# A mixing and decoding kernel: the first weights loaded in row halves, PSUM banks permuted, decode steps moved earlier, and VectorE making twelve casts in the first sweep

## What is computed

```
attn = einsum('ds,td->st', w1, w2) * sparse_mask
y    = gelu(einsum('bds,st->bdt', x, attn) + b2)        # exact gelu
x    = layernorm(x + y)
mask = norm(x) > 64                                     # per token
w_l, w_h = dequant(qweight, lut4, 4 bits), dequant(qweight, lut8, 8 bits)
x    = layernorm(x + where(mask, x @ w_h.T, x @ w_l.T) + bias)
```

## Time and profile before

| what | us |
|---|---|
| median of 3 runs | 336.0 (335.06 to 337.29) |
| the profiled execution | 336.07 |
| its span, first to last instruction | 334.3 |
| TensorE busy | 301.7 (90%) |
| VectorE busy | 194.5 (58%) |
| ScalarE busy | 185.5 (55%) |
| GpSimd busy | 104.3 (31%) |
| mean granted TensorE clock | 0.956 of full |

### The profile page before, as it was taken

One profiled execution on the slowest core, in us unless ns is written; L12 is line 12 of the kernel. 1 busy time (PEld: TensorE's weight loads), 2 busy tenths in 40 slices (PEclk: granted clock), 3 DMA queues, 4 the chain that ended last, 5 costly groups with the idle time before them and its releaser, 6 DMA issues.

```text
span 334.3 us, 5046 instructions
## 1 busy us (share of the span) xinstructions
PE 301.7 (90%) x1907; PEld 263.6 (79%) x1907; DVE 194.5 (58%) x347; ACT 185.5 (55%) x246; POOL 104.3 (31%) x179
## 2 busy tenths in 40 slices
PE   5899478989996779999999999999999999999970
PEld 2788375656664579999999999999999878878870
DVE  0668857436879577889966766640315434534361
ACT  1656653447887967897857887942124545121210
POOL 3000000322323237779888630000013232322220
PEclk9899877999997959999999999999999999999996
DMA  7999616799987592000111111111905877444232
GB/s 246 371 384 361 225 60 220 223 228 296 218 139 128 80 158 56 32 33 31 38 43 33 38 45 35 60 47 36 304 10 190 259 267 237 176 147 159 94 125 73
DMA packets 27183, 49.35 MB, mean 148 GB/s; under 512 B 2320, under 2 KB 11792, under 8 KB 27152
## 3 DMA queue, kind: packets, MB, share of 16 engines
q1 hardware_dynamic: 22800, 40.56, 35.0%
q0 software_dynamic: 4352, 8.39, 14.7%
HBM read 36.36 MB, written 12.58 MB: 146 GB/s over the span
## 4 chain that ended last, share of the span: by engine, by line
PE 64%; issue 12%; SPq 6%; POOL 6%; DMA 4%; DVE 3%; ACT 2%; POOLq 0%; DVEq 0%
PE acc L536 18%; PE acc L538 18%; PE acc L537 18%; POOL z L1329 5%; PE acc L519 4%; DMA q_low<-in_qbits 4%; SPq L250 3%; PE acc L461 2%; PE acc L451 1%; PE acc L415 1%; ACT x_hi L666 1%; SPq L254 1%; PE acc L431 1%; PE acc L433 0%; PE acc L432 0%
## 5 line engine op out<-in xcount | busy, mean ns | idle before, releaser
L536 PE MATMUL acc<-lin,zz 128*128 128x256 f32 (+2 forms) x424 | 130.9, 309 | 0.3 <-POOL lin L1337 0.3
L538 PE MATMUL acc<-lin,zz 128*128 128x256 f32 (+2 forms) x424 | 130.3, 307 | 0.0
L537 PE MATMUL acc<-lin,zz 128*128 128x256 f32 (+2 forms) x424 | 130.1, 307 | 0.0
L536 PEld LDWEIGHTS acc<-lin,zz 128*128 128x128 f32 x424 | 80.7, 190 | 4.7 <-issue 0.6
L537 PEld LDWEIGHTS acc<-lin,zz 128*128 128x128 f32 x424 | 80.8, 191 | 4.0
L538 PEld LDWEIGHTS acc<-lin,zz 128*128 128x128 f32 x424 | 80.7, 190 | 4.1
L692 ACT ACTIVATE leaf<-planes,lut,flip 128x1024 f32<-128x1024 uint8 x56 | 67.6, 1234 | 0.0
L948 DVE COPY_PREDICATED leaf<-planes,leaf 128x1024 f32<-128x1024 uint8 x32 | 43.1, 1346 | 12.5 <-ACT leaf L692 12.0
L1329 POOL DMA_DIRECT2D z<-in_xr x16 | 19.7, 1257 | 97.3 <-ACT z L674 97.3
L785 ACT ACTIVATE junk<-rows,cols 128x1024 bf16<-128x1024 f32 x15 | 17.2, 1149 | 41.3 <-POOL cols L1303 41.3
L415 PE MATMUL acc<-w,w 128*128 128x272 f32 (+1 forms) x128 | 31.5, 412 | 4.1 <-DMA w<-in_w1b 4.1
(11 more groups left out here) (105 smaller groups left out, 429.8 us busy)
## 6 DMA issues: line engine op xcount, KB each, us to landing
z<-in_xt SPq DMA_DIRECT2D x16, 512.0 KB, 8.8
z<-in_xr POOLq DMA_DIRECT2D x16, 512.0 KB, 6.9
out_rows<-rows SPq DMA_DIRECT2D x15, 512.0 KB, 2.9
w<-in_w2b SPq DMA_DIRECT2D x4, 1024.0 KB, 9.9
w<-in_w1b SPq DMA_DIRECT2D x8, 512.0 KB, 9.4
out_rows<-parts SPq DMA_DIRECT2D x32, 128.0 KB, 1.8
rows<-out_rows SPq DMA_DIRECT2D x16, 256.0 KB, 2.8
off_band<-in_mask_rest SPq DMA_DIRECT2D x8, 448.0 KB, 4.2
```

Source lines behind the costliest of these rows:

```text
L536: nc.tensor.matmul(bank, hi, w_hi, start=k == 0, stop=False)
L537: nc.tensor.matmul(bank, hi, w_lo, start=False, stop=False)
L538: last = nc.tensor.matmul(bank, lo, w_hi, start=False, stop=k == KB - 1)
```

## The change

- The first strip's weights (w2's first quarter, w1's block 0) are loaded in two halves of rows, and strip 0 begins with the first half. q_low is loaded as blocks 0 to 3 right behind the first half and blocks 4 to 7 after the second pair of x, instead of blocks 0, 1 and the rest. x of group 1 is loaded without the two waits.
- The mask band, the excess operands and the warm-up tile move to addresses 128 to 140 KiB, where lin's first part comes later; so lin_hi(0), lin_lo(0) and the memsets of ones wait for their last readers.
- The banks are permuted: units 0 to 3 use banks 4 to 7, units 4 to 7 banks 0 to 3, strips 2 and 3. The turned block 0 is in banks 0 and 1.
- The excess strip stands behind the turn of block 0, ahead of strip 7. Group 0 is mixed in the order of the others. Block 1 is turned behind group 3 and not inside it; later turns stand one or two tiles later. The squares run three tiles ahead at first.
- 24 decode steps stand in the strips (22 before), 9 in the mixing (12 before), 33 in the first sweep (32), 30 in the second. In a group they stand behind gelu 0 and gelu 3 on ScalarE, ahead of the x_lo of pair 0 and of pair 2 on VectorE.
- Group 0's z pairs are made in groups 2 and 3. VectorE makes x_hi of group 0's pairs 0 and 2, and z_hi of groups 1 to 3, in the first sweep's tiles 0 to 10, where before ScalarE made z_hi, six pairs of it in the mixing.

```diff
     EARLY_PARTS = 2 * TILES
-    STATS_AHEAD = 1
+    STATS_AHEAD = 3
...
     DECODE = LEAVES + 3
-    EARLY_STEPS = [5, 2, 2, 2, 2, 3, 3, 3]
-    UNIT_STEPS = [n % 2 for n in range(18)] + [1, 1, 1, 0, 0, 0]
-    FIRST_STEPS = [2] * TILES
-    MIX_Z = {(2, 0): (0, 0), (2, 2): (0, 1), (2, 4): (0, 2), (3, 0): (0, 3), (3, 2): (1, 0), (3, 4): (1, 1)}
-    FIRST_Z = [((1 + n // PAIRS, n % PAIRS),) for n in range(2, 3 * PAIRS)] + [()] * 6
-    SECOND_STEPS = [2] * 15 + [1]
+    EARLY_STEPS = [6, 3, 3, 3, 3, 3, 2, 1]
+    MIX_STEPS = [(2, 1), (2, 1), (1, 0), (2, 0)]
+    MIX_Z = {2: ((0, 0), (0, 1)), 3: ((0, 2), (0, 3))}
+    FIRST_Z = [((1, 0), (1, 1)), ((1, 2),), ((1, 3),)] + [((2 + n // PAIRS, n % PAIRS),) for n in range(2 * PAIRS)] + [()] * 5
+    FIRST_STEPS = [1] + [2] * 11 + [3, 2, 3, 2]
+    SECOND_STEPS = [2] * 15 + [0]
...
     TURN_AFTER_STRIP = 6
-    TURN_IN_MIX = {3: 1}
-    TURN_IN_FIRST = {4: 2, 9: 3, 15: 4}
+    TURN_IN_FIRST = {5: 2, 11: 3, 15: 4}
...
         eye = eye2[:, P:2 * P]
-        UNIT_BANKS, GRAM_BANKS, SUM_BANK = (0, 1, 2, 3, 4, 7, 5, 6), (4, 5), 7
-        STRIP_BANKS, EXCESS_BANK = (5, 6), 7
+        UNIT_BANKS, GRAM_BANKS, SUM_BANK = (4, 5, 6, 7, 0, 1, 2, 3), (4, 5), 7
+        STRIP_BANKS, EXCESS_BANK = (2, 3), 7
...
+            def load_first(rows, signal):
+                sp.dma_start(w2[:, rows, 0:D // W2_PARTS], w2b[0][:, rows, :]).then_inc(signal, 16)
+                sp.dma_start(w1[:, 0, rows, :], w1b[0][:, rows, :]).then_inc(signal, 16)
...
-            for n in range(W2_PARTS):
+            load_first(slice(0, KB // 2), w_first)
+            load_q(0, slice(0, HALF_BLOCKS))
+            sp.dma_start(lut[:, :, :], lut4).then_inc(tables_loaded, 16)
+            sp.dma_start(b2[:, :], b2c).then_inc(tables_loaded, 16)
+            load_first(slice(KB // 2, KB), w_loaded[0])
+            load_w2(1)
+            load_w1(1)
+            load_band(0)
+            load_w1(2)
+            for n in range(2, W2_PARTS):
...
                     load_w1(b)
-                    if b == 0:
-                        load_q(0, slice(0, 2))
-                        sp.dma_start(lut[:, :, :], lut4).then_inc(tables_loaded, 16)
-                        sp.dma_start(b2[:, :], b2c).then_inc(tables_loaded, 16)
-                        load_band(0)
             load_band(1)
-            load_x(0, 0)
...
             sp.dma_start(band_e[0:EXCESS, :, :, :], mask_e).then_inc(e_loaded, 16)
+            load_x(0, 0)
             load_xe(0)
-            load_q(1, slice(2, KB))
-            for r in range(1, PAIRS):
+            load_x(0, 1)
+            load_q(1, slice(HALF_BLOCKS, KB))
+            for r in range(2, PAIRS):
                 load_x(0, r)
-            load_x(1, 0)
-            sp.wait_ge(masked, KB)
-            load_x(1, 1)
-            sp.wait_ge(mix_e_step, 4)
-            for r in range(2, PAIRS):
+            for r in range(PAIRS):
...
             load_xe(1)
+            sp.wait_ge(mix_made, KB)
...
                     pe.wait_ge(masked, b - 1)
-                pe.wait_ge(w_loaded[b], 32 if b in [blocks[0] for blocks in W1_AFTER] else 16)
+                if b:
+                    pe.wait_ge(w_loaded[b], 32 if b in [blocks[0] for blocks in W1_AFTER] else 16)
+                else:
+                    pe.wait_ge(w_first, 32)
                 for d in range(KB):
+                    if (b, d) == (0, KB // 2):
+                        pe.wait_ge(w_loaded[0], 32)
...
                 else:
-                    if t < 2:
+                    if t in (4, 5):
...
                 if b == TURN_AFTER_STRIP:
-                    turn_early(0)
-            excess_strip()
-            for t in (2, 3, 0, 1):
-                own(0, t)
-            beside(0, 0)
-            beside(0, 2)
-            for t in (4, 5):
-                own(0, t)
-            beside(0, 1)
-            beside(0, 3)
-            own(0, 6)
-            beside(0, 5)
-            own(0, 7)
-            beside(0, 4)
-            beside(0, 6)
-            for g in range(1, GROUPS):
+                    pe.wait_ge(consts_made, 4)
+                    turn(0)
+                    excess_strip()
+            for g in range(GROUPS):
...
                 own(g, 7)
-                turn_in_mix(g)
...
                 beside(g, 6)
+            pe.wait_ge(gelu_done, KB * (GROUPS - 1) + 4)
+            turn(1)
...
             for j in range(TILES):
-                if j + STATS_AHEAD < TILES:
-                    tile_squares(j + STATS_AHEAD)
+                if STATS_AHEAD <= j + 1 < TILES:
+                    tile_squares(j + 1)
...
-                if g == GROUPS // 2 and r == 0:
-                    act.wait_ge(mixed, HALVES * GROUPS)
...
             for b in range(KB):
...
+                if b == KB - 2:
+                    make_x_hi(0, 1)
                 make_mix_hi(b)
-            for r in range(PAIRS):
-                make_x_hi(0, r)
-                if r == 1:
+                if b == KB - 3:
                     make_xe_hi(0)
+            make_x_hi(0, 3)
             make_lin_hi(0)
-            gelu(0, 0)
-            for t in range(1, KB):
-                gelu(0, t)
-                if t // 2 in X_ON_ACT and t % 2:
-                    make_x_hi(1, t // 2)
-                if t == 4:
-                    make_xe_hi(1)
-            for g in range(1, GROUPS):
-                for t in range(KB):
-                    gelu(g, t)
-                    if g + 1 < GROUPS:
-                        if t % 2 and t // 2 in X_ON_ACT:
-                            make_x_hi(g + 1, t // 2)
-                        if t == 2:
-                            make_xe_hi(g + 1)
-                    if (g, t) in MIX_Z:
-                        make_z_hi(*MIX_Z[g, t])
...
+            for g in range(GROUPS):
+                gelu(g, 0)
+                done = decode_steps(MIX_STEPS[g][0], done)
+                if g + 1 < GROUPS:
+                    make_xe_hi(g + 1)
+                gelu(g, 1)
+                if g + 1 < GROUPS:
+                    make_x_hi(g + 1, 1)
+                gelu(g, 2)
+                gelu(g, 3)
+                for pair in MIX_Z.get(g, ()):
+                    make_z_hi(*pair)
+                done = decode_steps(MIX_STEPS[g][1], done)
+                gelu(g, 4)
+                gelu(g, 5)
+                if g + 1 < GROUPS:
+                    make_x_hi(g + 1, 3)
+                gelu(g, 6)
+                if g + 1 == GROUPS:
+                    make_lin_hi(1)
+                gelu(g, 7)
...
             for j in range(TILES):
-                for g, r in FIRST_Z[j]:
-                    make_z_hi(g, r)
...
             def make_planes(b, part):
-                if b in (0, 2) and part == 0:
-                    dve.wait_ge(q_loaded[b // 2], 16)
+                if b in (0, HALF_BLOCKS) and part == 0:
+                    dve.wait_ge(q_loaded[b // HALF_BLOCKS], 16)
...
                 dve.wait_ge(lin_hi_made, b + 1)
+                if b == 0:
+                    dve.wait_ge(mix_e_step, 4)
...
                         merge(b, (2, 5, 6, 8, 10).index(i))
-                    if (b, i) == (2, 10):
-                        make_lin_lo(1)
...
+                dve.wait_ge(residual_done[r], 16 * (g + 1))
+                if g == GROUPS // 2 and r == 0:
+                    dve.wait_ge(mixed, HALVES * GROUPS)
+                nc.vector.tensor_copy(zz[:, 1, g, 2 * r:2 * r + 2, :], z[:, g, 2 * r:2 * r + 2, :]).then_inc(z_hi_made, 1)
...
                     make_mix_lo(b - 1)
-            make_x_lo(0, 0)
+                if b == KB - 3:
+                    make_x_lo(0, 0)
+                if b == KB - 2:
+                    make_xe_lo(0)
+                    make_mix_e()
+                    make_x_lo(0, 1)
             make_mix_lo(KB - 1)
-            make_x_lo(0, 1)
-            make_mix_e()
-            make_xe_lo(0)
+            make_x_lo(0, 2)
             make_lin_lo(0)
-            make_x_lo(0, 2)
             make_x_lo(0, 3)
-            for r in range(PAIRS):
-                make_x_lo(1, r)
-                if r == 2:
-                    make_xe_lo(1)
-            for g in range(1, GROUPS):
-                for t in range(KB):
-                    if g + 1 < GROUPS:
-                        if t % 2:
-                            make_x_lo(g + 1, t // 2)
-                        if t == 2:
-                            make_xe_lo(g + 1)
-                    if (g, t) in MIX_Z:
-                        make_z_lo(*MIX_Z[g, t])
...
+            for g in range(GROUPS):
+                done = decode_steps(MIX_STEPS[g][0], done)
+                if g + 1 < GROUPS:
+                    make_xe_lo(g + 1)
+                    make_x_lo(g + 1, 0)
+                    make_x_lo(g + 1, 1)
+                for pair in MIX_Z.get(g, ()):
+                    make_z_lo(*pair)
+                done = decode_steps(MIX_STEPS[g][1], done)
+                if g + 1 < GROUPS:
+                    make_x_lo(g + 1, 2)
```

(8 more changed lines are left out.)

83 lines of the change are left out of this document (35 added, 48 removed).

## The result

The changed kernel takes 325.43 us (median of 4 runs, 324.38 to 326.16) against 336.64 us for the kernel before on the same chip (4 runs, 335.06 to 338.91): a ratio of 0.966, 95% interval 0.959 to 0.973. Forecast were 323.5 us and a range of 317 to 331. The profiled execution took 324.97 us, its span 323.2: 11.1 us less than before, where 12.65 had been worked out.

The account below looks back on a forecast made before the run. TensorE was taken as the bound, hole-free from 121.20 us on; earlier stages would start squares 12 13.55 us sooner, less 0.9 for a moved turn: 336.07 - 12.65 = 323.4, said as 323.5 us, range 317 to 331.

Parts of the forecast that it names:

- the slots: Strips: rounds of decode merges and planes between masks; slots 2 to 5 were to take 18.5 us, to strip 5's mask.
- the new bound lies in the loop of ScalarE and VectorE: Strips: decode, not weights, sets the pace; a one-merge slot takes 3.78 us against 3.71 for a strip.
- about 2.4: Group 0: sign of being right, two TensorE waits of about 2.4 us, on mix_e and lin_lo.
- the term of 8.14 us from unit 4 to group 1: Group 0: the old kernel's 58.58 to 66.72, added to unit 4's 52.9 to start group 1 at 61.0.
- such a loss off at group 3: Mixing: old halved clock behind group 3's 2.75 us wait, 3.10 us at 0.50; 1.55 us taken off.
- Groups 1 to 3: Mixing: no waits, 39.7 us instead of 47.15, ending at 100.7.
- Handover: Group 3's end to tile 0's linear part: 4.85 us instead of 7.33, squares 2 waiting for VectorE's reading of squares 0.
- squares 12: First sweep: start of tile 12's squares, the event whose shift is forecast, at 152.0 instead of 165.55.
- a lower clock behind the first would be covered by the second: First sweep: slow clock after the 2.8 us wait costs nothing, since VectorE's sum sets the wait before squares 12.
- 0.6 us for disturbed casts: First sweep: extra time for twelve VectorE casts beside GpSimd, taken from a span of 0 to 3.4 us.
- slower rival: First sweep: each of twelve casts waits 1.6 us for GpSimd, 19 us more, 342 us; chance 0.04.
- its own 5.5 us for the casts: First sweep: casts on VectorE bring 4.9 us of new TensorE waiting, plus 0.6 for disturbance by GpSimd.

Follow-up runs that it names:

- codes-behind run: Changed kernel with q_low (codes of blocks 0 to 3), tables and b2 transferred behind both halves of the first weights: 327.48 us, ratio 0.975.
- two steps a slot: Changed kernel with two decode steps a strip instead of three, 21 in the strips, the last three moved to group 0: 325.53 us, ratio 0.970.
- codes first: Changed kernel with q_low, tables and b2 transferred ahead of the first half rows of weights: 326.61 us, ratio 0.973.
- the last section: The experiments; with the changed kernel's last three early decode steps moved to group 0, the clock was 0.54 from 117 to 120 us: 323.00 us.
- run with one tile ahead: Changed kernel with STATS_AHEAD 1 instead of 3, squares 2 issued behind tile 0's linear part: 324.12 us, ratio 0.966.

## Why the prediction was right, and where not

- **Strips.** The mask of strip 1 was over at 20.58 for 20.2, since q_low landed 1.32 us earlier (6.91 for 8.23) where 1.8 had been worked out; the slots took 18.56 us for 18.5, and the turn had no wait. The step "the new bound lies in the loop of ScalarE and VectorE" holds, shown by the codes-behind run (every microsecond passed on) and by two steps a slot. What the text left out is that the band and strip 1 lie within 2.5 us of that bound.
- **Group 0.** mix_e's matmul waited 2.10 us and lin_lo's 1.96, against "about 2.4". Unit 4 started at 53.78 for 52.9. Group 1 was to start at 61.0 and did at 63.06: the term of 8.14 us from unit 4 to group 1 came out at 9.28. The step that failed is this one: the halved clock behind the new wait, 3.22 us at 0.50, was not in the sum. It cost 1.56 us: with the codes first, where the clock is full there, the same stretch takes 7.72 us (53.88 to 61.60). It was left out although the forecast itself took such a loss off at group 3, and by the last section it can fall elsewhere.
- **Groups 1 to 3.** No wait, as forecast, and 38.92 us for 39.7 (63.06 to 101.98).
- **Handover.** 5.24 us for 4.85. The wait for the reading of squares 0 is there (0.78), behind lin_lo(1). The ones were ready at 106.65, close behind it; the run with one tile ahead shows them as the next limit.
- **Sweep.** Tile 0 to squares 12 took 46.07 us for 46.5; the waits were 2.62 and 1.85 for 2.8 and some 2. That a lower clock behind the first would be covered by the second is wrong; the profiled execution of the changed kernel merely had none there. The last section shows one that was passed on in full. The 0.6 us for disturbed casts was not needed: a cast took 0.690 at the median. The slower rival falls by the same row: GpSimd's instructions get longer, VectorE's casts don't. The rule of the Trainium skill ("SBUF — State Buffer", "SBUF: two separate sides"), an exclusive lock for a whole instruction, would fit GpSimd's 1.10 and 1.46 us beside VectorE's work. Of its other half, a cast that is blocked by GpSimd, these rows show nothing: least and longest cast lie 0.055 us apart.
- **Behind squares 12.** 169.91 us for 168.75 and the turn's 0.9; no new wait, as forecast.
- **The sum.** At squares 12 the kernel was 1.29 us later than forecast and behind them 0.26, together the 1.55 between 12.65 and 11.1. Up to squares 12 the stages were off by 0.9, 1.2, -0.8, 0.4 and -0.4 us, so the sum is a little better than its terms.

Right for its reasons, then, with one term missing: the forecast names the new waits and not the slow clock that follows one of them. The text took the casts on VectorE as a cost inside a gain, and that is what the experiment found: without them the kernel is at 320.7, where forecast less its own 5.5 us for the casts says 318. What the permuted banks alone are worth was not tried, since units, strips, turns and squares share them; nor were the place of the excess strip and the loads of x without their waits. Only the trace speaks for the banks: squares 0 start right behind the turn with no wait for a gelu.

## What to carry to other kernels

Before an engine is given more work, add up its whole queue between two fixed events: that sum said where and by how much TensorE would wait, and the idle time of the other engine, 20 of 46 us on ScalarE, said where the work belonged. When a transfer or an operation is moved forward, look at what else arrives just in time at the place where it is used; there were two such things at the masks of strips 0 and 1, and a gain needs all of them. And price a new wait on TensorE with the slow stretch that can follow it. That stretch was free only where TensorE had to wait for VectorE behind it anyway, and VectorE did not come to wait for TensorE in between.
